# Merged one-column operations on VectorE, the next-to-last projection moved behind the last gate and up, and 14 unread products on TensorE

## What is computed

```python
x = x + ssm(ctx_1024, layernorm(x), ...)          # state = state*dA + (d_t*u_t)*B_t ; y_t = sum_n state*C_t
q1 = activation_quant(layernorm(x))               # row: s = 127/clip(max|x|, EPS); round(x*s)/s
h  = silu(q1 @ ternary(w_gate).T) * (q1 @ ternary(w_up).T)     # 512 -> 2048
h  = ln_weight * h * rsqrt(mean(h*h) + RMS_EPS)
out = x + activation_quant(h) @ ternary(w_down).T              # 2048 -> 512
```

## Time and profile before

| | |
|---|---|
| time, median of 3 runs | 585.87 us (585.73 to 586.31) |
| the profiled execution | 586.31 us, its span 584.4 us, mean granted PE clock 0.991 |
| PE busy | 541.3 us, 93% |
| DVE busy | 540.5 us, 92% |
| ACT busy | 512.1 us, 88% |
| POOL busy | 464.5 us, 79% |

### The profile page before, as it was taken

The page is one execution under the profiler, slowest core; times in us unless marked ns, Lnnn a source line. Parts: engine busy times, 40 slices in busy tenths (PEclk is TensorE's granted clock), DMA queues, the critical chain, the costliest instruction groups (busy, mean ns, idle before and its releaser), DMA issues.

```text
span 584.4 us, 10287 instructions
## 1 busy us (share of the span) xinstructions
PE 541.3 (93%) x3667; PEld 404.7 (69%) x3684; DVE 540.5 (92%) x820; ACT 512.1 (88%) x755; POOL 464.5 (79%) x184
## 2 busy tenths in 40 slices
PE   5898987999999999999999888998889999999996
PEld 2335476899998989989999888995334444444442
DVE  3999979999999999999999999997998999999873
ACT  1899999999999999989999799998967868778673
POOL 4888374999999899999999999994564765666662
PEclk9999999999999999999999899899999999999998
DMA  9992690221112741127331194234532533424321
GB/s 285 407 364 73 230 309 11 56 65 64 55 55 91 163 117 65 59 63 202 88 98 55 55 228 168 62 128 106 104 65 63 109 81 78 112 65 97 94 54 55
DMA packets 62194, 68.65 MB, mean 117 GB/s; under 512 B 41136, under 2 KB 41136, under 8 KB 59968
## 3 DMA queue, kind: packets, MB, share of 16 engines
q1 hardware_dynamic: 59776, 63.59, 36.3%
q0 software_dynamic: 2368, 4.40, 4.5%
HBM read 50.02 MB, written 8.52 MB: 100 GB/s over the span
## 4 chain that ended last, share of the span: by engine, by line
DVE 28%; PE 26%; ACT 17%; POOL 12%; issue 11%; DMA 5%; SPq 0%; DVEq 0%; POOLq 0%; ACTq 0%
POOL arena L470 11%; ACT arena L682 8%; PE ps L1221 8%; PE ps L1205 6%; ACT arena L607 5%; DVE arena L808 5%; PE ps L1208 4%; PE ps L1263 4%; PE ps L1256 3%; DVE arena L897 3%; DVE arena L985 3%; DMA arena<-arena 2%; DVE bst_x L840 2%; DVE am L954 1%; DMA arena<-x 1%
## 5 line engine op out<-in xcount | busy, mean ns | idle before, releaser
L470 POOL TENSOR_TENSOR arena<-arena 128x2048 f32<-128x2048 f32 x63 | 286.4, 4592 | 13.2 <-DVE arena L897 11.1
L897 DVE TENSOR_TENSOR_SCAN arena<-arena,ps 128x512 f32<-128x512 f32 x256 | 286.7, 1197 | 2.0 <-ACT arena L682 0.5
L682 ACT ACTIVATE arena<-arena,a_neg 128x512 f32<-128x512 f32 x256 | 165.5, 712 | 9.5 <-DVE arena L897 9.2
L1221 PE MATMUL ps<-ident,arena 128*128 128x128 f32 x1024 | 156.0, 276 | 6.7 <-POOL arena L470 3.4
L1221 PEld LDWEIGHTS ps<-ident,arena 128*128 128x128 f32 x1024 | 121.2, 142 | 10.7 <-POOL arena L470 6.2
L504 POOL TENSOR_TENSOR arena<-arena 128x1024 f32<-128x1024 f32 x30 | 71.1, 2371 | 57.2 <-DVE arena L985 57.2
L1256 PE MATMUL ps<-arena 128*128 128x512 bf16 x504 | 112.9, 379 | 2.1 <-DVE arena L985 1.1
L1205 PE MATMUL ps<-arena 128*128 128x128 f32 x768 | 102.3, 276 | 3.4 <-ACT arena L607 2.1
L1208 PE MATMUL ps<-ident,arena 128*128 128x128 f32 x640 | 97.8, 277 | 5.2 <-DVE arena L897 2.9
L607 ACT ACTIVATE arena<-arena,bT 128x512 f32<-128x512 f32 x160 | 102.0, 711 | 0.0
L1205 PEld LDWEIGHTS ps<-arena 128*128 128x128 f32 x768 | 93.3, 192 | 5.2 <-ACT arena L607 2.3
(11 more groups left out here) (121 smaller groups left out, 578.1 us busy)
## 6 DMA issues: line engine op xcount, KB each, us to landing
arena<-w_all SPq DMA_DIRECT2D x16, 1024.0 KB, 9.2
arena<-c_rows SPq DMA_DIRECT2D x64, 256.0 KB, 3.2
arena<-x SPq DMA_DIRECT2D x4, 1024.0 KB, 15.8
w_ternary<-arena SPq DMA_DIRECT2D x8, 512.0 KB, 4.2
arena<-w_ternary SPq DMA_DIRECT2D x8, 512.0 KB, 5.0
arena<-x POOLq DMA_DIRECT2D x4, 1024.0 KB, 10.0
out<-arena SPq DMA_DIRECT2D x16, 256.0 KB, 2.0
arena<-ctx_t SPq DMA_DIRECT2D x4, 512.0 KB, 13.7
```

The source lines that it names most:

```text
L470: nc.gpsimd.tensor_tensor(hs[:, k % RING, :, :], hs[:, k % RING, :, :], c_bc[:, s:s + 1, :].to_broadcast([P, KE, L]), ALU.mult).then_inc(S ...
L682: nc.scalar.activation(dA[:, s, i, :], delta_u[:, b, 0, i, :], ACT.Exp, scale=a_neg[:, i, n:n + 1]).then_inc(S["dA_ready"], 1)
L897: nc.vector.tensor_tensor_scan(out=hs[:, k % RING, i, :], data0=dA[:, k % 2, i, :], data1=ps[:, 4 + i, :], initial=0.0, op0=ALU.mult, op1= ...
L1221: last = mm(ps[:, c, i * P:(i + 1) * P], hs[:, k % RING, i, c * P:(c + 1) * P], ident[:], start=(n == 0 and i == 0), stop=(n == DS - 1), i ...
```

## The change

Four things are changed.

1. DVE's one-column operations. The sum of squares is taken of the already scaled `h` (ACT's `Square` gets `scale=scales[...]`), so `variance` needs one operation for it instead of two, and the end of the program two instead of four. `scale_row` has four operations instead of six: one for both columns of `scales`, and a reciprocal that needs no factor behind it. In the network's loop `bias` is computed by POOL, right behind `power`.
2. PE's order at the end. `down(13)` stands behind `gate_and_up(15, 3)` instead of ahead of it. On ACT `silu(15, 3)` stands ahead of the scaling of tile 14, on DVE `gated_up(15, 3)` ahead of `biggest_end(0)` and the rounding of tile 14, and `scale_rows(13)` comes behind the scaling of tile 15.
3. The last output rows get a place of their own (`o_end`), so DVE's last operation does not wait for an earlier store.
4. `keep_array_warm` issues products of 128x512 that nothing reads: 6 in step 2 ahead of the wait for the first `q2T`, then 2, 4 and 2 around the transposes at the end.

The diff, without hunks that only repeat these (the `...` lines):

```diff
@@ gpsimd
+            def bias(t):
+                pool.wait_ge(S["rstd_ready"], t + 1)
+                hold(pool, "xn_ready", t)
+                nc.gpsimd.tensor_scalar(bia[:], mv[:, 0:1], rstd2[:, 0:1], -1.0, ALU.mult,
+                                        ALU.mult).then_inc(S["bias_ready"], 1)
...
             for t in FFN_STEPS:
                 if tile(t - 1) or tile(t + 3):
                     power(EARLY + t + 1, 0 if tile(t + 3) else 1, 2 if tile(t - 1) else 1)
+                if tile(t + 3):
+                    bias(t + 3)
@@ scalar
                     hold(act, "h_ready", t * 4, "ssq_ready", t - 1)
-                    nc.scalar.activation(sq_out, h2[:, 1 - s, :], ACT.Square,
+                    nc.scalar.activation(sq_out, h2[:, 1 - s, :], ACT.Square, scale=scales[:, t - 1, 1:2],
                                          accum_out=ssq[:, t - 1:t]).then_inc(S["ssq_ready"], 1)
...
+                if t == END:
+                    silu(t, 3)
                 if tile(t - 1):
                     hold(act, "aq_ready", t)
                     nc.scalar.activation(p2[:, 1 - s, :], p2[:, 1 - s, :], ACT.Identity, bias=magic[:],
                                          scale=aq[:, t - 1:t]).then_inc(S["tq_ready"], 1)
...
-                if tile(t):
+                if tile(t) and t < END:
                     silu(t, 3)
...
-                if tile(t - 2):
+                if tile(t - 2) and t < END:
                     scale_rows(t - 2)
...
+            scale_rows(END - 2)
             act.wait_ge(S["qT_psum"], 2)
@@ vector
                     step(nc.vector.bn_stats(bst[:], x_all[:, n, :]))
+                    hold(dve, "bias_ready", n)
                     own.done(nc.vector.bn_aggr(mv[:], bst[:]))
                 if chain is not None:
                     dve.wait_ge(S["ssq_ready"], chain + 1)
-                    own.done(nc.vector.tensor_scalar(var2[:, 1:2], ssq[:, chain:chain + 1], scales[:, chain, 1:2],
-                                                     1.0 / INNER, ALU.mult, ALU.mult))
+                    own.done(nc.vector.tensor_scalar(var2[:, 1:2], ssq[:, chain:chain + 1], 1.0 / INNER, RMS_EPS,
+                                                     ALU.mult, ALU.add))
                 own.wait()
                 if n is not None:
-                    own.done(nc.vector.tensor_scalar(var2[:, 0:1], mv[:, 1:2], LN_EPS, None, ALU.add))
-                if chain is not None:
-                    own.done(nc.vector.tensor_scalar(var2[:, 1:2], var2[:, 1:2], scales[:, chain, 1:2], RMS_EPS,
-                                                     ALU.mult, ALU.add))
-                own.wait()
+                    step(nc.vector.tensor_scalar(var2[:, 0:1], mv[:, 1:2], LN_EPS, None, ALU.add))
                 dve.sem_inc(S["var_ready"], 1)
...
-                step(nc.vector.tensor_scalar(am[:], am[:], Q_EPS, None, ALU.max))
-                own.done(nc.vector.reciprocal(s1[:], am[:]))
-                for w in range(2):
-                    own.done(nc.vector.tensor_scalar(scales[:, x, w:w + 1], wmean[:, w:w + 1], am[:], 1.0 / 127.0,
-                                                     ALU.mult, ALU.mult))
-                own.wait()
-                step(nc.vector.tensor_scalar(s1[:], s1[:], 127.0, None, ALU.mult))
-                dve.sem_inc(S["s1_ready"], 1)
+                step(nc.vector.tensor_scalar(am[:], am[:], Q_EPS, 1.0 / 127.0, ALU.max, ALU.mult))
+                step(nc.vector.tensor_scalar(scales[:, x, :], wmean[:, 0:2], am[:], None, ALU.mult))
+                nc.vector.reciprocal(s1[:], am[:]).then_inc(S["s1_ready"], 1)
...
-                if tile(t + 3):
-                    bias(EARLY + t + 1)
                 if tile(t):
                     gated_up(t, 2)
                 if t == END:
+                    gated_up(t, 3)
                     biggest_end(0, 0, 2)
...
-                gated_up(t, 3)
                 if t < END:
+                    gated_up(t, 3)
                     biggest(t, 0)
@@ tensor
+            def keep_array_warm(bank, n):
+
+                for _ in range(n):
+                    mm(ps[:, bank, :], q1T[:, 0, 0, :], wg[:, 0, 0:512], start=True, stop=True)
...
-                    if j == 2 and tile(t - 2):
-                        pe.wait_ge(qT_done[t % 2], ((t - 2) // 2 + 1) * 16)
+                    if j == 2 and t == 2:
+                        keep_array_warm(DOWN_BANK[0], 6)
+                    if j == 2 and tile(t - 2) and t < END:
+                        turned_by_dma(t - 2)
                         pe.wait_ge(S["wd_cut"], 4)
                         down(t - 2, 0, KI)
...
             pe.wait_ge(S["h_ready"], END * 4 + 2)
+            turned_by_dma(END - 2)
+            down(END - 2, 0, KI)
+            pe.wait_ge(S["h_ready"], END * 4 + 4)
+            keep_array_warm(G_BANK[0], 2)
             pe.wait_ge(S["q_ready"], END)
             turn_end(END - 1, ps_q, 0)
+            keep_array_warm(G_BANK[0], 4)
             pe.wait_ge(S["qT_copied"], 1)
             down(END - 1, 0, 8)
...
                 turn_end(END, ps_end(half), half * 8)
+            keep_array_warm(G_BANK[0], 2)
             pe.wait_ge(S["qT_copied"], 3)
             down(END, 0, 8)
```

28 lines of the change are left out of this document (12 added, 16 removed).

## The result

The changed kernel takes **590.60 us** (median of 6 executions, 590.20 to 591.32) where the kernel before takes 585.86 (6 executions, 585.44 to 586.31): ratio 1.0082, 95% interval 1.0069 to 1.0095. It is slower, and 580.3 was predicted. The span of the profiled execution is 588.7 us with a mean granted clock of 0.988.

The account below looks back on a forecast made before the run. DVE's in-order list was taken as the bound by 0.25 us a tile, PE right behind. Terms 2.0 + 1.74 + 0.5 + 0.4 + 1.65 + 0.15 - 0.15 - 0.2 = 6.1 us off 586.31 gave 580.2, stated as 580.3; range 578.8 to 582.8.

Parts of the forecast that it names:

- One-column operations: DVE's `scale_row` and `variance`: merging saves about 0.42 us a tile, taking DVE's list from 10.61 to 10.19 us, under PE's 10.36.
- Middle of the network, 2.0 us: Eight tiles of the network's loop step at PE's 10.36 us instead of taking 84.89 us together: 2.0 us saved.
- round trip: Rival, chance 0.06: q2, DMA, `down` with ACT's L754 set the middle's pace, not DVE's list; about 584 us.
- First `down` to second: Early network tiles: the step between two `down` falls from 12.10 to 10.36 us, 1.74 saved, if the transfer takes 4.35.
- That the long one comes again: The 5.93 us transfer recurring: some 1.5 us lost; part of the first rival, 581.5 to 582.3 us, chance 0.22.
- Scan stage, 0.4: Last batch ahead of the scan that POOL waited for: the same three DVE operations get shorter, saving 0.4 us.
- First tiles, 0.5: Start of the network, where PE waits for DVE or the DMA: DVE's savings count at once, 0.5 us (0.2 to 0.8).
- The end, 1.65 + 0.15 - 0.2: Last tiles: `down(15)` starts 1.65 us earlier, merged operations add 0.15, `Square` with a scalar operand costs 0.2.
- The clock's share: At the end: of the 1.65 us, 1.35 comes from `down(14)` running at full clock alone.
- an end at 0.50 in spite of the unread products: Cold-end rival, chance 0.12: `down(14)` takes 5.3 us again and the 1.65 us are lost; 582.0 us.
- Unread products: On PE, 0.216 us each: the first six, 1.3 us, lie in PE's wait of 1.55; the others fill the end.
- POOL's `bias`: Behind `power` on POOL: costs between nothing and 0.55 us in the first tile; 0.15 taken.

Follow-up runs that it names:

- E7: Kernel before with the merged one-column operations alone, `scales` by two one-column operations, `bias` on DVE, old end, no unread products: 582.24 us, ratio 0.9940.
- E6: E1 without the 14 unread products: 582.65 us, ratio 0.9953 to the kernel before.
- E9: E6 with `norm(t + 3)` on ACT moved ahead of the wait for `aq`: 582.31 us, ratio 0.9945 to the kernel before.
- E11: E6 with `bias` back on DVE behind `scale_row`: 581.50 us, ratio 0.9936 to the kernel before.
- E1: Changed kernel with `scales` made by two one-column operations instead of one of two columns: 582.57 us, ratio 0.9965 to the kernel before.
- E4: Changed kernel with one-column `scales` operations for the scan stage's three tiles, the two-column one in the network's loop: 583.33 us, ratio 0.9970 to the kernel before.
- E12: E9 with all 14 unread products in it again: 582.29 us, ratio 0.9952 to the kernel before.
- E10: E6 with the six operations of the old `scale_row`: 583.67 us, ratio 0.9978 to the kernel before.
- E2: Kernel before with one edit, `scales` by one two-column operation instead of two one-column ones: 592.35 us, ratio 1.0101.
- E8: Kernel before with the new end alone, including its unread products of 2, 4 and 2: 584.81 us, ratio 0.9992.
- E3: Changed kernel with `scales` as three columns instead of two, the third not read: 590.76 us, ratio 1.0099 to the kernel before.
- E5: Changed kernel with both columns of `scales` in one `tensor_tensor` instead of the `tensor_scalar`: 586.79 us, ratio 1.0017 to the kernel before.

## Why the prediction was wrong, by its steps

**The step that failed** is in "One-column operations": "one of about 0.24 (an operation of two columns and a scalar operand; I take 0.21 + 0.03)". Two one-column operations were replaced by one of another kind, and it was priced by the rows of the old kind. The operations of DVE in rows 4 are one-column, read PSUM (L985), or ran behind the end of POOL's product (L1033, at 482.75; POOL's L504 had ended at 481.72). No row showed a two-column one beside POOL, and neither end of its cost was bounded. An upper bound near enough stood in rows 5: two products of POOL take 9.10 us. The operation took 5.38, and the stage lost 7.5 us where 0.4 was to be gained. The prediction looked at what POOL waits for and never asked what POOL holds. None of the rivals had this in it.

**Middle of the network, 2.0 us: wrong, 0.8 measured** (E7: 8 steps at 10.51 instead of 10.61). "DVE has next to no idle time there that another engine ends: its in-order list [...] is the 10.61 us" took coincidence for cause. The ring through ACT was as long as the list. Taking 0.5 us out of `scale_row`, which is not on the ring, turned it into a wait of 0.41 for the `Square`; only the 0.18 of `variance`, less 0.09 of the slower `Square`, counted. The rival "round trip", given 0.06, named nearly the right mechanism, with ACT's L754 in it; but the way goes over `aq`, `Square` and the variance, not over the DMA.

**First `down` to second (the prediction says third to fourth), 1.74 us: right** in E6, E7, E9 and E11 (10.37 instead of 12.10). "That the long one comes again is not for the change to decide" was wrong: in all six traces with the six unread products it came at the seventh tile, in the four without them and with the merged `scale_row` it did not come, and in the four with the old `scale_row` it came at the second. The traces also show what goes with it. Fourteen traces have 196 of these transfers (`turn_q`). Ten took 5.81 to 6.07 us, three 4.93 to 5.21, all others 4.25 to 4.53. In the thirteen, and in no other, a load of instructions (a DMA queue of its own, 16 KB in the ten, 8 KB in the three) starts 3.4 to 4.1 us behind the issue of the transfer. The DMA view of before over the load at 433.90 and of the changed kernel over that at 493.32:

```profile
q8 instruction: 1, 0.02, 5.3%
```

```profile
q8 instruction: 1, 0.02, 5.2%
```

The transfers were issued at 430.0 and 489.3. At the seventh tile of E6, without unread products, the load starts at 486.94, when the transfer issued at 481.6 has landed; in E1 it starts at 486.35 and meets the one issued at 482.7. So a change of the program moves the loads against the transfers. That the load is the cause is not shown by a run of its own, but nothing in the fourteen traces speaks against it.

**Scan stage, 0.4: not shown.** Where the stall is absent, it is there in E7 and E4 (67.02 and 67.00 instead of 67.42), nothing in E1, E9, E11 and E12 (67.43 to 67.46), and 0.5 the other way in E6 and E10 (67.92 and 67.91). The scatter of single executions is as large as the term. **First tiles, 0.5**: 0.15 to 0.4, but in E9 and E12 the first `down` came 0.2 later than before, and in E10 0.1.

**The end, 1.65 + 0.15 - 0.2: right in sum**, 1.70 after and 1.72 in E1, in part by luck. The clock's share held: E2 has the old end and happened to run it at full clock, in 31.12 us instead of 32.44, 1.32 for the clock alone (1.35 predicted); E10 has the new order and 0.50 granted, and gained nothing (32.50). But the order alone gave 0.09 (E8 against E2) where 0.3 was counted, and the merged operations 0.31 where 0.15 less 0.2 was. And since the old end ran at full clock in E2, the 1.32 are there only against an execution like the profiled one of before. What the unread products do is less settled. In the seven traces with them the clock never fell at the end; in the seven without them it fell in three (before, E7, E10) and not in four, three of which (E6, E9, E11) have the same work on PE there as E10. That fits a guard worth 1.3 us in some executions. It is not shown to be one.

The prediction read rows 8 wrong. The same view of before has these groups beside the one shown there:

```profile
L1205 PE MATMUL ps<-arena 128*128 128x128 f32 x30 | 4.1, 277 | 0.0
L1221 PE MATMUL ps<-ident,arena 128*128 128x128 f32 x24 | 3.6, 273 | 0.0
```

L1208, the eleven, are transposes, and so by its form is L1221 (`is_transpose`); the ordinary products are the thirty of L1205. So rows 8 say nothing against the Trainium skill (TensorE: Matmul & The Clock Gate, Part 4) on work in transpose mode. What that rule was made to forecast here, an end at 0.50 in spite of the unread products, came in none of the seven traces.

**Unread products: "lie in PE's wait" was right** for the first six, but the seventh tile's long transfer, and with it 0.7 us (E6 to E1) and 0.9 (E9 to E12), came with them. **POOL's `bias`** took 0.27 us, not 0.55, hidden, and gained nothing.

Summed for E1, in traces: 0.0 + 0.24 + 1.88 + 1.72 = 3.8 us of the 6.1 predicted, and its median is 2.4 us under that of before. In the changed kernel the 7.5 us stand against 3.1.

The changed kernel also loses 0.67 us in the network against E1; E4, with the held operation in the loop, doesn't. Its trace has three short halts of DVE that no engine ends, up to 456.23, 498.32 and 541.31. In the waits of DVE from 424 to 560 us they read (us in total, times, longest):

```profile
DVE arena L985 <- issue: 0.8, 3, 0.3
```

Two of the steps between `down`, 10.70 and 10.73 us, follow on the first and the last. E3 and E5 have the same three halts and lose 0.59 and 0.41; none of the other eleven traces has one.

What stays open: what held the operation in the 0.47 us ahead of POOL's product, how a load of instructions lengthens a transfer, why DVE halts, and what decides about the clock at the end from execution to execution.

## What to carry to other kernels

Merging small operations changes their kind: ask of each new one what it reads and writes through, and bound it by the longest instruction of the engine that shares the way, here POOL's product of nearly 5 us (the stall was 0.5 longer still). A stall on a shared port shows as a long operation, so compare the durations of one group (min, median, max) before you look for waits. And an engine without waits is not yet the bound: follow one value once around the loop, add up both lists, and see whether two of them end together.

## What the runs showed of the hardware

A DVE operation over 2 or 3 fp32 columns, 256 or 384 numbers in all, took up to 5.4 us and ended with a GpSimd product of 128x2048, as `tensor_scalar` and as `tensor_tensor`. A one-column operation (L960) and a reduction over 512 columns (L959) right ahead of it were not held in any of the sixteen tiles (153 to 155 and 658 to 687 ns). The bn_aggr that writes two columns (L928) was not held either: 181 to 184 ns in 16 tiles, 14 of them under a GpSimd operation. The large conversion into bf16 (L1034), 1.22 to 1.23 us in 14 tiles, took 1.47 in the one where a GpSimd operation ran beside it, for its first 0.38 us. A transposing transfer of 4.4 us took 5.8 to 6.1 where a 16 KB load of instructions started 3.4 to 4.1 us into it, in ten of ten cases.
